# A mixture-of-experts stage in a fused attention kernel: weight differences moved ahead, gate rows by products, gate table in halves

## The reference

```python
logits = tokens @ router_w.T
topv, topi = jax.lax.top_k(logits, K)             # K = 2 of 8 experts
w = jax.nn.softmax(topv, axis=-1)
gate = zeros((T, n_experts)).at[arange(T)[:, None], topi].add(w)
for e in range(n_experts):
    h = jax.nn.gelu(tokens @ w1[e].T, approximate=False)
    out = out + gate[:, e:e + 1] * (h @ w2[e].T)
x = x + tanh(g_ffn[0]) * out
```

## Time and profile before

| | us |
|---|---|
| median of 3 runs | 167.25 |
| the three runs | 161.99, 167.25, 167.89 |
| the profiled execution | 162.34 |
| its span | 160.6 |
| PE busy | 125.8 (78%) |
| DVE busy | 122.9 (77%) |
| ACT busy | 86.1 (54%) |
| POOL busy | 37.2 (23%) |

### The profile page before, as it was taken

The page is one execution under the profiler, slowest core; times in us unless marked ns, Lnnn a source line. Parts: engine busy times, 40 slices in busy tenths (PEclk is TensorE's granted clock), DMA queues, the critical chain, the costliest instruction groups (busy, mean ns, idle before and its releaser), DMA issues.

```text
span 160.6 us, 2047 instructions
## 1 busy us (share of the span) xinstructions
PE 125.8 (78%) x642; PEld 86.7 (54%) x642; DVE 122.9 (77%) x346; ACT 86.1 (54%) x152; POOL 37.2 (23%) x59
## 2 busy tenths in 40 slices
PE   6999879798898688898999956899999930008892
PEld 4677555373365456656666534778675820006650
DVE  4986897134169999999866765788838899999893
ACT  3335474325529458867778055416345499491480
POOL 1003202020503050849500039742201000000000
PEclk9999996899999999999999999999999998555999
DMA  4991000000074123031200000000000000000003
GB/s 144 349 414 45 2 0 0 0 0 0 8 230 168 52 81 119 11 131 42 89 4 0 0 0 0 2 0 4 2 0 0 0 0 2 0 0 4 0 0 131
DMA packets 3101, 8.17 MB, mean 51 GB/s; under 512 B 265, under 2 KB 1289, under 8 KB 2834
## 3 DMA queue, kind: packets, MB, share of 16 engines
q1 hardware_dynamic: 3088, 8.03, 14.3%
q10 hardware_dynamic: 2, 0.00, 0.0%
HBM read 7.48 MB, written 0.56 MB: 50 GB/s over the span
## 4 chain that ended last, share of the span: by engine, by line
PE 38%; DVE 28%; issue 15%; ACT 10%; DMA 3%; POOL 2%; POOLq 1%; DVEq 0%; ACTq 0%; SPq 0%
PE bank L1145 6%; PE bank L1141 5%; PE bank L1142 4%; PE bank L1118 4%; DVE hidden L834 3%; DVE low_parts L841 3%; PE bank L1257 3%; PE bank L1125 2%; DVE amax_u L995 2%; DMA q_exp<-gates 2%; PE bank L1269 2%; DVE amax_g L995 2%; DVE hidden L1029 2%; DVE amax_p L1000 2%; ACT wexp L601 2%
## 5 line engine op out<-in xcount | busy, mean ns | idle before, releaser
L1118 PE MATMUL bank<-zero 128*128 128x256 f16 x168 | 25.3, 301 | 16.8 <-ACT ng L597 15.1
L1118 PEld LDWEIGHTS bank<-zero 128*128 128x128 f16 x168 | 17.4, 108 | 21.3 <-ACT ng L597 15.5
L495 ACT ACTIVATE hidden<-bank 128x512 f32<-128x512 f32 x32 | 18.9, 593 | 7.7 <-PE bank L1145 7.3
L366 POOL TENSOR_TENSOR we_lo<-wexp,we_hi 128x512 fp32r<-128x512 f32 (+1 forms) x8 | 12.8, 1607 | 37.7 <-ACT we_hi L453 30.4
L841 DVE TENSOR_TENSOR low_parts<-hidden,high_parts 128x512 fp32r<-128x512 f32 x20 | 15.3, 765 | 2.3 <-ACT high_parts L501 2.2
L501 ACT ACTIVATE high_parts<-hidden 128x512 fp32r<-128x512 f32 x20 | 12.6, 632 | 8.3 <-DVE hidden L834 8.0
L1141 PE MATMUL bank<-xhi,we_hi 128*128 128x512 f32 x32 | 15.1, 472 | 1.2 <-ACT xhi L437 1.2
L834 DVE TENSOR_TENSOR hidden<-hidden,q_soft 128x512 f32<-128x512 f32 x16 | 12.4, 785 | 4.7 <-ACT q_soft L513 3.5
L1145 PE MATMUL bank<-xlo,we_hi 128*128 128x512 f32 x32 | 12.9, 402 | 1.0 <-DVE xlo L726 1.0
L353 POOL TENSOR_TENSOR rstd<-var,neg_half 128x4 f32<-128x4 f32 x6 | 6.1, 1018 | 29.1 <-DVE var L637 29.1
L1142 PE MATMUL bank<-xhi,we_lo 128*128 128x512 f32 x32 | 12.6, 394 | 0.0
(11 more groups left out here) (242 smaller groups left out, 291.6 us busy)
## 6 DMA issues: line engine op xcount, KB each, us to landing
wexp<-in_experts SPq DMA_DIRECT2D x2, 1024.0 KB, 8.1
q_exp<-gates SPq DMA_DIRECT2D x3, 512.0 KB, 3.5
q_soft<-gates SPq DMA_DIRECT2D x3, 512.0 KB, 3.6
wq<-in_lpbq SPq DMA_DIRECT2D x1, 576.0 KB, 10.0
stream<-in_x SPq DMA_DIRECT2D x2, 256.0 KB, 3.4
xn<-gates SPq DMA_DIRECT2D x1, 512.0 KB, 5.7
out<-hidden SPq DMA_DIRECT2D x2, 256.0 KB, 2.0
pa<-in_packa SPq DMA_DIRECT2D x1, 325.0 KB, 3.5
```

What stands on the lines that cost most here:

```text
L366: pool.tensor_tensor(w_lo[e][:, cols], raw(e)[:, cols], w_hi[e][:, cols].bitcast(f32), ALU.subtract)\
L495: act.activation(ge[u % NB][:, :], bank[4 + u % NB][:, :], ACT.Gelu).then_inc(gelu_done, 1)
L1118: mm(bank[b][:, 0:256], zero16[:, 0:128], zero16[:, 0:256], start=True, stop=True)
```

## The change: what it does

- **Weight differences**: `high_weights` 2 and 3 move on ACT to the place of 0 and 1, and 4 to 7 are spread over ACT's list ahead of the steady loop. POOL builds the head mask first, then differences 0 and 1, and 2 and 3 once the gates of the first half are there (`gate_ready` 1), and 4 to 7 once those of the second half are (`gate_ready` 2). The steady loops of ACT and POOL hold none.
- **Expert 1's gate rows**: `second_gate` no longer reads `gateT`. For each of four token tiles PE takes the gate column of expert 1, broadcast to 128 columns, as stationary operand, and the identity as moving one (four fp32 products of 128 columns). It now stands ahead of `gate_columns` of its half.
- **Gate table in halves**: SP stores each half of the table when it is there, and reads expert 2's row of that half at once (`third_in`); the store of the second half stands behind both steps of the first.
- **First units**: `first_pair(h)` runs the products with the token high parts of both chunks of expert 0, then waits for the token differences, then the two that need them. `Z_ORDER` is 0, 1, 4, 5, 2, 3, and units 4 and 5 are projected ahead of the second half's transposes. `low_tokens(0)` moves ahead of `add_attention(1)` on DVE. Three groups of filler products stand inside `logits`, of two for the first half and one for the second.
- **DVE's order**: `gate_unit` 4 and 5, then `top_two(1)` and `gates_of(1)`, then the two steps on the keys; `weight_scales` moves from unit 9 to unit 7.
- **End**: PE's transposes of the first half's sum (`experts_to_tokens(0)`) move ahead of `y_unit(31)`.

```diff
-        Z_ORDER = [0, 1, 4, 2, 5, 3] + list(range(6, UNITS))
+        Z_ORDER = [0, 1, 4, 5, 2, 3] + list(range(6, UNITS))
...
             for h in range(HALVES):
                 sp.wait_ge(gateT_ready[h], 1)
-            sp.dma_start(gates[:, :], gateT[:, :]).then_inc(gates_out, 16)
-            sp.wait_ge(gates_out, 16)
-            for e in range(2, EXPERTS):
-                if e >= 3:
-                    sp.wait_ge(gated, (e - 2) * HALVES * FC)
+                sp.dma_start(half(gates, h), half(gateT, h)).then_inc(gates_out[h], 16)
+                sp.wait_ge(gates_out[h], 16)
+                sp.dma_start(half(gate_rows[0], h), half(gates, h)[2:3, :].broadcast_to([128, HT]))\
+                    .then_inc(third_in[h], 16)
+            for e in range(3, EXPERTS):
+                sp.wait_ge(gated, (e - 2) * HALVES * FC)
...
+            low_weights(0)
+            low_weights(1)
+            rstd_of(3)
+            rstd_of(4)
+            pool.wait_ge(gate_ready, 1)
+            low_weights(2)
+            low_weights(3)
+            pool.wait_ge(gate_ready, 2)
             for e in range(4, EXPERTS):
-                pool.wait_ge(gated, FIRST * (e - 3) + 1)
                 low_weights(e)
...
             gelu(0)
+            gelu(1)
             gate_tanh(0)
-            gelu(1)
             normalise(x2, 4)
             gelu(4)
             evac(half(xhi, 1), bank[1][:, :], xT_mm, 4, xhi_ready)
-            high_weights(2)
-            gate_columns(0)
-            gelu(2)
             second_gate(0)
             gelu(5)
+            high_weights(4)
+            gelu(2)
             gelu(3)
+            high_weights(5)
+            gate_columns(0)
             gate_tanh(1)
-            high_weights(3)
+            high_weights(6)
             gelu(6)
+            second_gate(1)
+            gate_columns(1)
+            high_weights(7)
             gelu(7)
-            gate_columns(1)
-            second_gate(1)
...
+            low_tokens(0)
             add_attention(1)
-            low_tokens(0)
...
-            gate_unit(FIRST)
-            for u in range(FIRST, UNITS):
+            gate_unit(4)
+            gate_unit(5)
+            n = top_two(1)
+            gates_of(1, n)
+            keys_sum()
+            keys_softmax(steps[0])
+            for u in range(5, UNITS):
...
+            def first_pair(h):
+                pe.wait_ge(we_split, 1)
+                pe.wait_ge(xhi_ready, h + 1)
+                for u in range(FC * h, FC * h + FC):
+                    k = slice(u % FC * D, (u % FC + 1) * D)
+                    mm(bank[4 + u][:, :], w_hi[0][:, k], half(xhi, h), start=True, stop=False)
+                    mm(bank[4 + u][:, :], w_lo[0][:, k], half(xhi, h), start=False, stop=False)
+                pe.wait_ge(xlo_ready, h + 1)
+                for u in range(FC * h, FC * h + FC):
+                    k = slice(u % FC * D, (u % FC + 1) * D)
+                    mm(bank[4 + u][:, :], w_hi[0][:, k], half(xlo, h), start=False, stop=True).then_inc(z_ready, 1)
...
             def second_gate(h):
 
-                pe.wait_ge(gateT_ready[h], 1)
-                mm(bank[2 + h][:, :], ident[0:EXPERTS, 1:2].broadcast_to([EXPERTS, 128]), half(gateT, h),
-                   start=True, stop=True).then_inc(first_rows_mm, 1)
+                pe.wait_ge(lg_read, h + 1)
+                pe.wait_ge(gate_ready, h + 1)
+                for t in range(TILES):
+                    last = mm(bank[2 + h][:, t * D:(t + 1) * D],
+                              gate_[:, h * TILES + t, 1:2].broadcast_to([128, 128]), ident[:, :],
+                              start=True, stop=True)
+                last.then_inc(first_rows_mm, 1)
 
             pe.wait_ge(exp_in[0], 16)
-            z_unit(0)
+            first_pair(0)
             pe.wait_ge(rw_ready, 1)
             pe.wait_ge(k1_ready, 2)
             logits(0)
-            z_unit(1)
             y_first(0)
             y_first(1)
+            z_unit(4)
+            z_unit(5)
             normalised(bank[1], 4)
-            z_unit(4)
-            z_unit(2)
+            second_gate(0)
+            first_pair(1)
             logits(1)
             gate_columns(0)
-            z_unit(5)
-            z_unit(3)
-            second_gate(0)
             y_first(2)
             y_first(3)
             z_unit(6)
+            second_gate(1)
+            gate_columns(1)
             z_unit(7)
-            gate_columns(1)
-            second_gate(1)
             for u in range(FIRST, UNITS):
+                if u == UNITS - 1:
+                    experts_to_tokens(0)
                 y_unit(u)
```

More of the change, by code:

```diff
@@ L245, in build @@
         gateT_ready = [sem(f"gateT_ready{h}") for h in range(HALVES)]
-        gates_out, first_rows_mm = map(sem, ("gates_out", "first_rows_mm"))
+        gates_out = [sem(f"gates_out{h}") for h in range(HALVES)]
+        third_in = [sem(f"third_in{h}") for h in range(HALVES)]
+        first_rows_mm = sem("first_rows_mm")
         rows_in = [sem(f"rows_in{odd}") for odd in range(2)]
@@ L322, in _ @@
                 sp.wait_ge(gateT_ready[h], 1)
-            sp.dma_start(gates[:, :], gateT[:, :]).then_inc(gates_out, 16)
-            sp.wait_ge(gates_out, 16)
-            for e in range(2, EXPERTS):
-                if e >= 3:
-                    sp.wait_ge(gated, (e - 2) * HALVES * FC)
+                sp.dma_start(half(gates, h), half(gateT, h)).then_inc(gates_out[h], 16)
[4 more added lines that the diff above has]
+                sp.wait_ge(gated, (e - 2) * HALVES * FC)
                 sp.dma_start(gate_rows[e % 2][:, :], gates[e:e + 1, :].broadcast_to([128, TOKENS]))\
                     .then_inc(rows_in[e % 2], 16)
-                if e == 2:
+                if e == 3:
                     sp.dma_start(first_gate, gates[0:1, :].broadcast_to([128, TOKENS])).then_inc(first_in, 16)
@@ L367, in low_weights @@
                     .then_inc(we_split, 1)
[L369 to L376, removed]
             link(pool.memset(head_mask[:, :, :], 1.0))
@@ L477, in _ @@
             evac(half(xT, 1), bank[7][:, :], xT_mm, 2, xT_ready)
-            high_weights(0)
-            high_weights(1)
+            for e in range(4):
+                high_weights(e)
             evac(v1[:, :, 0:D], bank[2][:, 256:512].rearrange("p (h d) -> p h d", d=D), kv1_mm, 2, k1_ready)
@@ L546, in _ @@
                     gelu(u + 2)
-                if u % FIRST == 0 and u // FIRST + 2 < EXPERTS:
-                    high_weights(u // FIRST + 2)
                 if u in (23, 25, 27):
@@ L818, in _ @@
             low_tokens(1)
-            n = top_two(1)
-            gates_of(1, n)
             def gate_unit(u):
@@ L826, in gate_unit @@
                     dve.wait_ge(second_rows, h + 1)
+                elif e == 2:
+                    dve.wait_ge(third_in[h], 16)
                 elif u % FIRST == 0:
-                    dve.wait_ge(rows_in[e % 2], 16 * (e // 2))
+                    dve.wait_ge(rows_in[e % 2], 16 * ((e - 1) // 2))
                 if u >= 2 * FIRST:
@@ L854, in _ @@
                     low(u)
[L855 to L860, removed]
+                if u == 7:
                     weight_scales()
@@ L1238, in logits @@
                                  True, True)
+                    if t < TILES - 1:
+                        keep_warm(1, 2 - h)
                 last.then_inc(lg_mm, 1)
@@ L1250, in z_unit @@
                 three(bank[4 + u % NB][:, :], w_hi[e][:, k], w_lo[e][:, k], half(xhi, h), half(xlo, h),
-                      True, True, (xlo_ready, h + 1) if u < FIRST else None).then_inc(z_ready, 1)
+                      True, True).then_inc(z_ready, 1)
+            def first_pair(h):
[9 more added lines that the diff above has]
+                    mm(bank[4 + u][:, :], w_hi[0][:, k], half(xlo, h), start=False, stop=True).then_inc(z_ready, 1)
             def y_first(u):
@@ L1268, in y_unit @@
                     pe.wait_ge(gated, u - FIRST + 1)
+                    if e == 1:
+                        pe.wait_ge(gateT_ready[h], 1)
                     last = mm(bank[2 + h][:, :], raw(e)[:, k], hm[u % NB][:, :], start=start, stop=stop)
@@ L1288, in gate_columns @@
             def gate_columns(h):
-                pe.wait_ge(lg_read, h + 1)
-                pe.wait_ge(gate_ready, h + 1)
+                pe.wait_ge(second_rows, h + 1)
                 for t in range(TILES):
@@ L1339, in key_products @@
                     last.then_inc(kv_mm, 1)
-            experts_to_tokens(0)
             pe.wait_ge(const_late, 1)
```

2 lines of the change are left out of this document (removed).

## The result

| | us |
|---|---|
| median of the changed kernel, 4 runs | 154.99 (153.81 to 155.86) |
| median of the kernel before, 4 runs | 164.73 |
| ratio | 0.9543, 95% interval 0.9459 to 0.9628 |
| profiled execution after, and its span | 155.86, 154.1 |

The forecast range, 153.3 to 162.4, holds the time, and the sign was right; the single number, 159.4, lies 4.4 too high. The four runs of the kernel before are 161.99, 162.21, 167.25 and 167.89 us, and the ratio leaves the upper ones out: 162.34 x 0.9543 is 154.9, so the change is worth **7.4 us** (6.0 to 8.8 by the interval), where the prediction had 7.8.

What follows compares the result with a forecast made beforehand. VectorE was taken to bound the first part of the steady loop, begun late by the gate table's DMA, and TensorE the last. The second sum 7.8 us earlier, off the 167.25 median, gave 159.4; range 153.3 to 162.4.

Steps and rivals of the forecast that it cites:

- The two parts of the 7.8: Second sum of the experts 7.8 us earlier, 81.75 against 89.58: gain up to low 8's end, and gain behind it.
- First half and fillers: Before the first router: TensorE's 1.01 us wait ends sooner, six fillers cost 0.12 each, gates at 28.0 against 27.9.
- Clock: Whole fp32 units y_first(0) and (1): no fall of TensorE's clock, full 1.7 us gained; bounds 1.7 and 0.
- Second half's tokens: ACT's copy to xhi runs 28.85 to 29.45, 1.9 us earlier, because unit 4 is projected earlier.
- Second router: Gates of the second half at 35.9, 3.3 us earlier, with ACT's tanh no longer queued behind gelus.
- Unit 4: TensorE starts unit 4 at 39.15 against 43.13, 4.0 us earlier.
- Table: Gate table's 5.3 us of DMA leave the path; loading a half takes 2.0 to 3.54, taken as 2.7.
- Low 8: VectorE's low 8 done at 46.6: 45.3 without GpSimd, plus 1.3 us of lock-out by its differences and constants.
- Low 8 to the second sum: From 40.0 us, off come 1.9 weight_scales, 2.9 stretched steps, 0.7 constants, leaving 34.5; moved transposes add 0.65.
- The step that failed is the last: Whole time: 7.8 us carried over to the median of three runs, 167.25, giving 159.4; profiled execution 154.5.
- The rivals: Clock falls again, 160.9, chance 0.16; lock or late row costs more, 162.2, 0.12; steady part not shorter, 163.9, 0.09.
- The slower case: GpSimd's ten us in one block from 35.9 hold VectorE for their whole length: 168.3 us, chance 0.03.

Runs made afterwards that it cites:

- e1: The changed kernel without the nine filler products inside the logits: median 154.94 us, ratio 0.952 to the kernel before.
- e9: The kernel before with the nine filler products inside the logits and nothing else: median 165.84 us, ratio 1.004.
- e8: The kernel before with only the weight differences and their high parts moved out of the steady loop: median 163.06 us against 164.73.
- e3: The changed kernel with high parts and differences of experts 4 to 7 back in the steady loops of ScalarE and GpSimd: median 158.74 us, ratio 0.975.
- e2: The changed kernel with the transposes of the first half's sum back behind the last expert unit: median 154.12 us, ratio 0.939.
- e4: The changed kernel with the gate table stored whole and expert 2's row read whole: median 158.36 us, ratio 0.970.
- e5: The changed kernel with GpSimd's constants ahead of its first weight difference: median 154.06 us, ratio 0.946.
- e12: The kernel before with only low_tokens(0) moved ahead of add_attention(1) on VectorE: median 162.95 us, ratio 0.998.

## Why the prediction was right, point by point

- **The two parts of the 7.8.** Forecast were 2.9 us up to the end of low 8 and 4.9 from there to the second sum. Measured from the mark they are 5.1 (32.16 less 27.06) and 4.2 (39.96 less 35.73). That the sum came near the 7.4 of the ratio is partly luck: 2.2 too little in front, 0.7 too much behind, and a late mark. No experiment takes back the order of the first units or of VectorE's list, so most of the first part is read from the two timelines and not shown by an edit.
- **First half and fillers.** `xlo` came 1.05 earlier from the mark (3.85 against 4.90), TensorE no longer stood for it, and the gates of half 0 came no earlier to speak of (10.14 against 10.26). The fillers were priced at 0.12 each and cost 0.46 for nine. That they guard the clock was wrong (e1, e9).
- **Clock.** The 1.7 us were over-sized: it costs 1.33 on the path (e8). The prediction took the modelled end, 28.9, for the end of the two units, and the half of 3.45 for their length; by starts they took 3.21 (25.49 to 28.70) and in e8 2.00. Without the fall 8.0 of the 9.33 are left; how often the unprofiled runs of the kernel before have it is not known.
- **Second half's tokens.** 1.9 earlier was forecast; from the mark it is 10.95 (31.11), against 13.27: 2.3, with the clock in it.
- **Second router.** 3.3 earlier was forecast; measured 4.2 (37.53 less 20.16, against 39.07 less 17.46). From copy to gates it took 2.38, forecast 2.4, so the tanh wait went as said. What was mis-sized is ahead of it: the second logits with their fillers took 1.38 and not 1.7, the four fp32 products 0.94 (from 30.91 to 31.85) and not 1.16.
- **Unit 4.** 4.0 forecast, 5.0 measured, mostly for the same reasons.
- **Table.** Off the path, as said. The load of a half took 3.3 us, near the upper end of the range; gate 8 waited for its gelu, and gate 10 for nothing.
- **Low 8.** The lock was forecast at 1.3. Gates 6, 7 and the softmax step were stretched by 1.4 in their room, low 8 and the step behind it by 0.27 each. The Trainium skill's rule (SBUF — State Buffer, section "Who interferes with whom") fits: the two sides exclude each other. But e3 goes beyond a lock held for one instruction: there a GpSimd step was kept from its work for 9 us over a whole row of VectorE steps. What decides the price here is who is dense: before the steady part VectorE has gaps and both get through, in it GpSimd starves.
- **Low 8 to the second sum.** 35.15 forecast (34.5 and 0.65), 35.7 measured (47.22 to 82.95). The 0.65 of the transposes was 0.60 (e2).
- **The step that failed is the last**: carrying the gain over to a median of 167.25. The median of three was a poor guide: with a fourth run it is 164.73. The fall of the clock at 26 us doesn't tell the runs near 167 from the others, since the profiled execution of 162.34 has it. The one profile of this kind of run is that of e9, 167.85 us, the kernel before with fillers: its span is 5.5 longer than that of the kernel before, 2.85 of it ahead of the mark, 0.93 in the stretch (fillers) and 1.72 behind the second sum, where the clock fell. So such a run can consist of a late mark and a later fall, neither of which the change is seen to touch, and the 7.8 had to be taken from a like execution: from the profiled one the forecast was 154.5, and the measured median is 154.99.

The rivals: the clock did not fall in the changed order's profile; the lock cost less than 1.3; the steady part did shorten. The slower case, GpSimd holding VectorE for its whole length, did not come, and e3 shows that the danger lay the other way round, in a GpSimd that can't start.

## What to carry to other kernels

Before moving work from a second engine ahead of a loop, or leaving it there, ask whether the loop leaves that engine any turn: a list of VectorE steps with two SBUF operands and no gap made a 1.3 us GpSimd step last 10.5 (e3), and whoever needs its result pays. Compare two profiles from a mark inside them and not by their spans, and take out what the clock did. When one engine reads 100% busy, look at what the next one has left before pricing a saving: here 3 us of VectorE's work were worth 0.9.

## What was not expected of the hardware

- TensorE's first products kept their double length up to 5.5 us in one execution and up to about 10.8 in others, with the same list and TensorE busy nearly all the while; this alone moves a time by up to 2.9 us. The granted clock reads 1.00 there in all of them, so the cause is open.
- Stands of TensorE in the loop, one of 3.03 us (e3) and two of 1.49 and 1.64 (e4), went with some 6 us at a granted clock of 0.50, which began within the stand, and the stretch grew by 5.96 and 5.37, more than the stands.
- One GpSimd step of 1.27 us took 10.55 beside VectorE steps that lost nothing.
- Behind the second sum the clock also fell between 88 and 108 us in the profiles of e5, e9 and e12 and in few of the others, and this part was up to 1.9 us longer there.
